# Softmax attention and routed experts: products of two groups of probabilities issued together

## The reference

```python
x = x + attn(layernorm(x))           # 16 heads of 16 features
x = x + experts(layernorm(x))        # 8 experts, each token goes to 2 of them

# in attn, per head, beside a linear-attention memory mixed in by a gate:
scores = einsum('bhqd,bhkd->bhqk', q, k) * scale
attn   = einsum('bhqk,bhkd->bhqd', softmax(scores, axis=-1), v)
# in experts, per expert:
y = einsum('etf,ehf->eth', silu(g) * u, down_w)     # F = 688
```

## Time and profile before

| | us |
|---|---|
| median of 3 runs | 421.46 |
| the profiled execution's own time | 423.56 |
| its span in the trace | 421.4 |
| PE busy | 397.6 (94%) |
| DVE busy | 253.2 (60%) |
| ACT busy | 207.0 (49%) |
| POOL busy | 126.3 (30%) |
| PE, the last step's exponential ends | 267.2 |

### The profile page before, as it was taken

How to read it: one execution, slowest core, us unless ns; L and a number is a source line. 1 busy time by engine, 2 the same in 40 slices (tenths; PEclk the granted TensorE clock), 3 DMA queues, 4 the chain that set the end, 5 groups by cost and what they waited for, 6 DMA issues and landing times.

```text
span 421.4 us, 7005 instructions
## 1 busy us (share of the span) xinstructions
PE 397.6 (94%) x2418; PEld 227.8 (54%) x2419; DVE 253.2 (60%) x509; ACT 207.0 (49%) x395; POOL 126.3 (30%) x124
## 2 busy tenths in 40 slices
PE   8999989989999999899999799999999999999992
PEld 3464652223222322432332123699899998998991
DVE  6898889878888797679879601187233232222310
ACT  4428937676676777647566698621111121212110
POOL 6328874040301104012035240203823112321412
PEclk9999999999999999999999999999999999999997
DMA  7336924557340706203014169620454121312242
GB/s 234 109 114 111 286 41 88 93 143 239 107 169 9 264 0 206 79 5 131 2 30 158 50 188 391 185 84 27 147 140 58 31 39 27 51 27 37 27 125 25
DMA packets 22908, 45.05 MB, mean 107 GB/s; under 512 B 4464, under 2 KB 15600, under 8 KB 22032
## 3 DMA queue, kind: packets, MB, share of 16 engines
q0 software_dynamic: 9216, 30.28, 25.3%
q1 hardware_dynamic: 13184, 14.00, 12.9%
q10 hardware_dynamic: 480, 0.39, 0.3%
HBM read 23.76 MB, written 15.59 MB: 93 GB/s over the span
## 4 chain that ended last, share of the span: by engine, by line
PE 72%; DVE 12%; SPq 4%; DMA 4%; issue 2%; ACT 2%; another core or an unknown queue 1%; POOL 1%; DVEq 0%; POOLq 0%; ACTq 0%
PE psum L1382 68%; DVE mem L1086 6%; DMA mem<-mem 3%; SPq L471 2%; DMA mem<-x 1%; SPq L468 1%; ACT mem L902 1%; SPq L498 1%; PE psum L1533 1%; PE psum L1665 1%; PE psum L1559 1%; DVE mem L1151 0%; PE psum L1577 0%; DVE mem L1264 0%
## 5 line engine op out<-in xcount | busy, mean ns | idle before, releaser
L1382 PE MATMUL psum<-mem 128*32 128x512 f32 (+13 forms) x2286 | 387.2, 400 | 14.3 <-DVE mem L1086 3.9
L1382 PEld LDWEIGHTS psum<-mem 128*128 128x128 f32 (+7 forms) x2286 | 214.3, 144 | 174.9 <-issue 71.0
L1086 DVE TENSOR_REDUCE mem<-psum 128x1 f32<-128x1024 f32 x128 | 152.2, 1218 | 30.6 <-PE psum L1382 29.0
L902 ACT ACTIVATE mem<-psum 128x512 f32<-128x512 f32 x256 | 137.3, 605 | 62.3 <-PE psum L1382 59.5
L920 ACT ACTIVATE mem<-psum 128x384 f32<-128x384 f32 (+3 forms) x32 | 15.1, 471 | 75.8 <-PE psum L1382 70.9
L733 POOL DMA_INDIRECT sum_d<-mem x17 | 26.7, 1570 | 69.7 <-ACT mem L928 41.3
L691 POOL DMA_DIRECT2D mem<-gate_up x21 | 15.2, 729 | 106.9 <-DMA mem<-mem 106.9
L1251 DVE COPY mem<-mem 128x3 f32<-128x3 f32 x18 | 3.0, 168 | 59.5 <-PE psum L1665 53.9
L1264 DVE TENSOR_TENSOR mem<-mem,psum 128x384 f32<-128x384 f32 (+3 forms) x32 | 16.8, 527 | 27.3 <-ACT mem L923 25.3
L928 ACT ACTIVATE mem<-psum,mem 128x256 f32<-128x256 f32 x18 | 8.5, 473 | 37.4 <-PE psum L1382 37.4
L709 POOL DMA_INDIRECT xg_d<-mem x16 | 15.8, 985 | 7.2 <-issue 4.5
(11 more groups left out here) (129 smaller groups left out, 189.4 us busy)
## 6 DMA issues: line engine op xcount, KB each, us to landing
xg_d<-mem POOLq DMA_DIRECT2D x8, 1036.0 KB, 9.7
mem<-gate_up POOLq DMA_DIRECT2D x8, 688.0 KB, 4.4
mem<-gate_up POOLq DMA_DIRECT2D x8, 624.0 KB, 6.4
mem<-down POOLq DMA_DIRECT2D x4, 1024.0 KB, 9.7
mem<-mem SPq DMA_DIRECT2D x54, 64.0 KB, 2.8
mem<-mem SPq DMA_DIRECT2D x18, 128.0 KB, 4.6
mem<-xg_d SPq DMA_DIRECT2D x16, 129.5 KB, 2.4
mem<-x SPq DMA_DIRECT2D x4, 256.0 KB, 4.7
```

The costliest lines, as they stand in the source:

```text
L902: nc.scalar.activation(prob[:, t % 8], psum[:, score_bank(n, t)], ACT.Exp, scale=HD ** -0.5).then_inc(exp_ready, 1)
L1086: V.tensor_reduce(mx[:, par, k:k + 1], banks(2 * (k % 2), 2), AX.X, ALU.max).then_inc(max_ready, 1)
L1382: return nc.tensor.matmul(*a, **k)
```

## The change

- At steps 9, 17, 25, ... PE issues the products of two groups one behind the other, 8 products in place of 4 (from step 216 on at 219, 227, ..., and one group at step 255).
- The probabilities have 12 places: 8 as before, and 4 in `prob_end`, in the first 2048 words of the experts' area. `PLACE` gives each group of four its place, and `place_free` the count of products that ACT waits for.
- That area is free for weights only when all products are done. So the experts' places go by `GU = [1, 2, 3, 4, 5, 6, 0, 7]`: expert 6 takes place 0 and is loaded after step 255, behind the last down weights. Expert 3's load moves behind the fourth unit.
- `TURN` goes from 9 to 13 and `RETURN` from 15 to 19, `osb_copy` from step 3 to step 5, and everything in `POST` and `SIDE` 4 steps later. Bank 7 is missing at steps 11 to 18 in place of 7 to 14. `PEEL` goes from 11 to 15.

```diff
-PEEL = 11
+PEEL = 15
...
+        prob_end = words(G, 4, HALF)
...
-        TURN, RETURN = 9, 15
+        TURN, RETURN = 13, 19
...
-            12: (0, "combT", 0), 13: (0, "copy", 0), 14: (0, "combT", 1), 15: (0, "copy", 1),
+            16: (0, "combT", 0), 17: (0, "copy", 0), 18: (0, "combT", 1), 19: (0, "copy", 1),
...
+        PLACE = [0, 1, 2, 1]
+
+        def prob_of(n):
+            place, k = PLACE[n // 4 % 4], n % 4
+            return prob_end[:, k] if place == 2 else prob[:, 4 * place + k]
+
+        def place_free(t):
+
+            g = t // 4
+            return max(g - 1 if g % 2 else g - 3, 0)
+
+
+        GU = [1, 2, 3, 4, 5, 6, 0, 7]
+
+        def weights_of(e):
+            return gu[:, GU[e]]
...
         def needs(g):
 
-            return E if any(TILES[GATED[n]][1] == E - 1 for n in range(g + 1)) else E - 1
+            return 1 + max(TILES[GATED[n]][1] for n in range(g + 1))
...
             def load_gate_up(e):
 
-                pool.wait_ge(mrow_in, 64 * (e + 2))
-                if e == NQ:
+                pool.wait_ge(mrow_in, 64 * min(e + 2, UNITS))
+                if e == NQ - 1:
 
                     pool.wait_ge(q_in, 16 * GROUPS * UNITS)
-                for to, src in gate_up_pieces(gu[:, e], gu_d[:, e]):
+                if e == E - 2:
+                    pool.wait_ge(av_ps, 8 * UNITS)
+                for to, src in gate_up_pieces(weights_of(e), gu_d[:, e]):
                     pool.dma_start(to, src).then_inc(gu_in, 16)
...
             for u in range(NQ):
-                load_gate_up(u)
+                if u < NQ - 1:
+                    load_gate_up(u)
...
+            load_gate_up(NQ - 1)
             load_gate_up(NQ)
...
             scatter(0)
-            load_gate_up(NQ + 2)
...
             load_down((3, 5))
+            load_gate_up(E - 2)
             reciprocal_root(slice(4, 8), 6)
...
-                if t % 4 == 0 and t >= 8:
-                    act.wait_ge(av_ps, 16 * i + t // 4 - 1)
+                if t % 4 == 0 and place_free(t):
+                    act.wait_ge(av_ps, 16 * i + place_free(t))
                 act.wait_ge(sct_ps, n + 1)
-                nc.scalar.activation(prob[:, t % 8], psum[:, score_bank(n, t)], ACT.Exp,
+                nc.scalar.activation(prob_of(t), psum[:, score_bank(n, t)], ACT.Exp,
                                      scale=HD ** -0.5).then_inc(exp_ready, 1)
-                if r == 3 and t > 3:
+                if r == 5 and t > 5:
                     osb_copy(u - 1, (t // STEPS - 1) % 2)
...
-                if t > 1 and t % 4 == (3 if isinstance(n, int) and n >= TAIL else 1):
+                if t > 3 and t % 8 == (3 if isinstance(n, int) and n >= TAIL else 1):
+                    product(i, t // 4 - 2)
+                    product(i, t // 4 - 1)
+                if isinstance(n, int) and n == ALL - 1:
                     product(i, t // 4 - 1)
```

More of the change, by code:

```diff
@@ L373, in block_kernel @@
-        SIDE = {NQ * STEPS + n: w for n, w in {
[L374 to L379, removed]
+            16: (0, "combT", 0), 17: (0, "copy", 0), 18: (0, "combT", 1), 19: (0, "copy", 1),
@@ new lines, in block_kernel @@
+            20: (0, "wo", 0), 23: (0, "wo", 1),
+            STEPS + 16: (0, "xn2T", 2), STEPS + 17: (0, "copy", 2), STEPS + 18: (0, "xn2T", 3),
+            STEPS + 19: (0, "copy", 3), STEPS + 21: (0, "logits", 0),
+            STEPS + 31: (0, "rank", 0),
+            3 * STEPS + 17: (1, "combT", 0), 3 * STEPS + 19: (1, "copy", 0),
+            3 * STEPS + 23: (1, "wo", 0), 3 * STEPS + 27: (1, "wo", 1)}.items()}
+        SIDE = {NQ * STEPS + n: w for n, w in {
+            21: ("add", 0), 23: ("stats", 0), 25: ("add", 1), 27: ("stats", 1), 31: ("stats", 2), 33: ("stats", 3),
+            35: ("spread", 0), 37: ("norm", 0), 39: ("norm", 1), 41: ("norm", 2), 43: ("norm", 3),
+            45: ("norm", 4), 47: ("norm", 5), 49: ("norm", 6), 51: ("norm", 7),
+            STEPS + 23: ("best", 0), STEPS + 25: ("index", 0), STEPS + 27: ("chosen", 0),
+            STEPS + 29: ("weights", 0), STEPS + 33: ("slots", 0), STEPS + 35: ("slots", 1),
+            STEPS + 37: ("base", 0)}.items()}
@@ L575, in _ @@
                         e = sp.value_load(ex_i[0:1, bass.ts(i, 1)], min_val=0, max_val=E - 1)
-                        for to, src in gate_up_pieces(gu[:, 0], gu_d[:, bass.ds(e, 1)].rearrange("p o b f -> p (o b) f")):
+                        for to, src in gate_up_pieces(weights_of(0), gu_d[:, bass.ds(e, 1)].rearrange("p o b f -> p (o b) f")):
                             sp.dma_start(to, src).then_inc(more_in, 16)
@@ L759, in _ @@
             scatter(1)
-            for to, src in gate_up_pieces(gu[:, E - 1], gu_d[:, E - 1]):
+            for to, src in gate_up_pieces(weights_of(E - 1), gu_d[:, E - 1]):
                 pool.dma_start(to, src).then_inc(gu_in, 16)
@@ L1516, in product @@
                 for j in range(4):
-                    ins = mm(psum[32 * j:32 * j + 32, 6], vst[:, g // 8 % 2, kb, j], prob[:, (4 * g + j) % 8],
+                    ins = mm(psum[32 * j:32 * j + 32, 6], vst[:, g // 8 % 2, kb, j], prob_of(4 * g + j),
                              start=(kb == 0), stop=(kb == 7), skip_group_check=True)
@@ L1646, in columns @@
                     for b in range(HB):
-                        ins = mm(psum[0:m, 2 * half + up, k * n:(k + 1) * n], gu[:, e, b, c:c + m], xgT[:, par, b, 0:n],
+                        ins = mm(psum[0:m, 2 * half + up, k * n:(k + 1) * n], weights_of(e)[:, b, c:c + m], xgT[:, par, b, 0:n],
                                  start=(b == 0), stop=(b == HB - 1))
```

## The result

The changed kernel takes **431.63 us** (median of 4 runs, 430.76 to 432.60), the kernel before beside it on the same chip 421.53 (4 runs, 421.41 to 422.15). The ratio is 1.0242 with a 95% interval of 1.0227 to 1.0256, so 10.1 us more. The forecast was 430.7 us, 9.2 more.

The account below looks back on a forecast made before the run. The prediction took PE to set the pace, with DVE close behind. Attention terms 0.6 + 3.1 + 1.4 + 0.6 + 0.3 + 3.2 gave +9.2 us on 421.46, so 430.7 us; its own range was 428 to 433.

Parts of the forecast that it names:

- The saving per block, 0.22 us: On PE, two groups' products in one block save one way in and out: 0.22 us per 8 steps.
- Two waits per plain cycle, 6.15 to 6.17 us: In 8 steps without turning or mixing, PE waits 0.47 and 0.26 us for DVE's reductions to release banks, 0.49 us more net.
- Unit 25.8, turnings 25.8 apart: Attention units 1 to 3 take 25.8 us each against 24.8, 1.0 us more per unit.
- Unit 0 +0.6: The first attention unit, with no turning and no mixing in it, takes 0.6 us more.
- Units 4 and 5, +1.4 and +0.6: These attention units lose 1.4 and 0.6 us; the tables' extra DVE work already makes DVE the bound in some cycles.
- Last unit +3.2: Last attention unit, `score_t` alone: four cycles of 4.77 us against 3.93, 3.3 us, a little given back: 3.2 us more.
- both full: In the last unit before the change, PE (1.95 us) and ACT (1.92 us) are both fully busy per 4 steps.
- What costs nothing: Later post and side steps, 12 places, later `osb_copy` and moved expert loads add nothing; experts' stage stays 154 us.
- The rival in which expert 6's load is in the way: On POOL's queue, expert 6's load delays the second scatter: 4 us on top, 434.7 us; chance 0.05.
- that PE gains and nothing waits: Rival for attention: PE's saving comes through without waits, 7.0 us less, 414.4 us; chance 0.07.
- that waits and savings cancel: Rival for the attention cycles: one wait of 0.26 us per cycle instead of both, 421.5 us; chance 0.03.
- That the last unit costs nothing: Rival: ACT catches up on four banks during the projections, other units cost as worked out, 427.5 us; chance 0.10.

## Why the prediction was right, point by point

- **The saving per block, 0.22 us:** right. The block lasts 1.85 us, and where DVE is out of the way 8 steps take 0.19 less. The Trainium skill (TensorEngine Tiling (Array Packing), Key Properties) says that a change of tiling mode drains TensorE; the trace agrees as far as this goes, since 0.2 us is what one change less gives back. The warning of the Trainium skill (TensorEngine Tiling (Array Packing), PSUM Bottleneck) that tiling doesn't speed up the reading of PSUM, which may become the bottleneck, had the right sign, and shorter reductions do take the loss away in units 1 to 3. The trace agrees only in part: DVE is idle 1.57 us in each cycle, so its rate is not the limit. What makes PE wait is that rate together with two pairs of banks.
- **Two waits per plain cycle, 6.15 to 6.17 us:** right, 6.19 to 6.22. PE waits at pairs 3 and 4 as walked, 0.47 and 0.24 us where 0.47 and 0.26 were worked out. Shown by the halved reductions for units 1 to 3.
- **Unit 25.8, turnings 25.8 apart:** 25.8, 26.3 and 26.0 us; the turnings are 25.9 and 26.3 apart. Units 2 and 3 are 0.2 to 0.3 us above the walk.
- **Unit 0 +0.6:** wrong, 0.0. Halved reductions bring it from 24.44 to 23.9 us with either order, so DVE sets its pace already; that leaves PE nothing to lose is a reading that no run tests by itself.
- **Units 4 and 5, +1.4 and +0.6:** 4 was right (+1.5). For 5 the term was too small by 1.0 us. What the walk didn't have is the stretch at half clock of 1.35 us; without it (in the run with blocks up to step 215) the unit stands at +0.2 against the kernel before, so the walk's own +0.6 was too large by 0.4.
- **Unit 6 +0.3:** +0.9 between two executions, in a unit that varies by over 2 us by itself. Nothing follows from it.
- **Last unit +3.2:** right in kind, too large: +2.6 against the kernel before by PE's starts, +1.9 by ACT's, and 1.55 shown alone. Blocks were to be 4.77 us apart; they start at 249.04, 253.82, 259.09, 264.06 and 268.84, so 4.78 to 5.27. The old side of the sum was wrong. It took 3.93 us per 8 steps from the last few and +0.84 for each of four cycles. By ACT's starts the kernel before needs 4.3, 4.6, 6.1 and 4.0 us for the four runs of 8 steps, and the changed kernel 5.3, 4.8, 5.0 and 5.9. The step that failed here is "both full", read from the last 4 us and applied to the whole unit.
- **What costs nothing:** right. 154.5 us from the last exponential to the end, against 154.2 and 154.6 in the two profiles before. The rival in which expert 6's load is in the way is out. That the later turning gains 0.2 to 0.5% (on the third chip not clear of nothing for the turning alone) was not foreseen; it means that blocks themselves cost more than the difference of the two kernels, about 11 us on the third chip (434.62 - 423.47).
- **The rivals:** that PE gains and nothing waits is refuted in its condition, and that waits and savings cancel by the plain cycle, 6.2 us against 5.68. Pair 3's banks would have to be free 0.88 us after a reduction's start, and only with halved reductions are they (0.69 and a restart of 0.13, 0.82 us). That the last unit costs nothing is refuted by the run with blocks in the tail alone.

The errors of the terms partly cancel: -0.6 (unit 0), +0.4 (units 1 to 3), +0.1 (unit 4), +1.0 (unit 5), +0.6 (unit 6), -0.6 (last unit) leave 0.8 us but for rounding, the distance from the forecast's +9.2 to the +10.0 of the traces and, near enough, to the +10.1 of the medians. So the mechanism is right in the units that carry most of the sum, and that the total comes within 1 us is in part luck. 1.35 us of the +10.0 are a stretch at half clock that the forecast doesn't have, and unit 6's share lies within what that unit varies by.

## What to carry to other kernels

An order of work that saves the engine in front a few tenths per block can cost more at the engine behind it, although that one is idle 40% of the time: count how many buffers it has, and walk one cycle with four durations (first arrival, repeat, release, issue) before batching. A longer batch on the engine that produces needs more buffers or a faster reader. Here halved reductions made two pairs of banks enough in units 1 to 3; four pairs of banks were not tested. If a forecast rests on "this engine is full now", check it over the whole stretch and not at its end.

## What was not expected of the hardware

- **A stretch of 3.4 us at half the granted clock in the middle of a busy kernel.** It stood at 220.2 and 220.5 us in two executions of the changed kernel. PE had an idle gap of 1.32 us at 211.6 to 212.9 us before it, but the trace with blocks up to step 215 has the same gap and no such stretch:

```profile
212.92 0.63 PE L1601 MATMUL psum<-mem 128*128 128x128 f32 x4 [1.32 <-DVE mem L1151]
```

```profile
213.01 0.63 PE L1601 MATMUL psum<-mem 128*128 128x128 f32 x4 [1.32 <-DVE mem L1151]
```

  With halved reductions one begins at 212.8 us, while PE has been issuing without a break since 208.03. The four runs of the changed kernel that gave 431.63 us all have a mean granted clock of 0.992, as the profiled one with the stretch has; the two profiles of the kernel before have 0.995 and no stretch. But it doesn't belong to blocks alone: over the unchanged kernel's runs on the three chips the mean goes from 0.984 to 0.997, and the turning at step 13 has a stretch on the second chip. The cause is open.
- **Unit 6 takes from 22.3 to 26.6 us, whatever the kernel.** While POOL scatters rows, ACT stands idle for up to 2.38 us before an exponential. In part of that time PE is still to write the scores. In the longest case (the turning at step 13, second chip) the `score_t` starts at 236.01 us and its exponential at 238.67, where 0.43 us lie between them in the earlier trace rows, and the chain of waits names no engine for it:

```profile
235.76 0.60 ACT mem L902
236.36 2.32 another core or an unknown queue
238.69 0.59 ACT mem L902
```

  There the granted clock then fell for 3.5 us (239.3 to 242.8) after PE had stood for 2.27 us. What holds ACT back was not found, and no run was made for it.
